# Moving the logits ahead of the second normalisation, and the slot statistics into the attention loop, in a fused Perceiver layer

## The chip, the cores and the metric

The kernel runs on one core of a Trainium2 chip. The metric is the time of one execution on the device, in microseconds (us); less is better. A core has a matrix engine (PE), a vector engine (DVE), an activation engine (ACT), a general engine (POOL) and a sync engine (SP) that only issues transfers. Each engine runs its own list of instructions in order, and they meet through semaphores.

## The reference, cut to what matters

One layer on x (128 rows of 256), with a context of 12544 rows of 256, in fp32:

```python
x = x + xattn(layernorm(x), ctx, W, b)          # softmax attention over 12544 context rows
x = x + conv(layernorm(x), proj_w, proj_b, filter_time)   # two stages of Fourier convolution and gating
x = x + soft_moe(layernorm(x), ...)
# soft_moe: a second layernorm on its input, with norm_g, norm_b
xn = (z - mean(z)) * rsqrt(var(z) + 1e-5) * norm_g + norm_b
se = ((s - mean(s)) * rsqrt(var(s) + 1e-5) * slot_g + slot_b) * scale     # 1024 slot rows of 256
logits = xn @ se.T                               # 128 x 1024
dispatch, combine = softmax over rows, softmax over slots
slots = dispatch.T @ xn                          # 1024 x 256
eout = (gelu(slots @ Wg + bg) * (slots @ Wu + bu)) @ Wd + bd     # 16 experts, 64 slots each
out = combine @ eout
```

## The kernel before, in words

The work has four stretches, one after the other.

The start (to about 10 us): x is normalised (`norm(0)`), transposed (`xhT`), W.T W is formed (`WW`), and the query `q_hi`, `q_lo` comes out of both. fp32 values are split in a high and a low part so that PE can use its fast fp32r form.

The attention loop: the context comes in 25 groups of 4 tiles of 128 rows (`raw`). Per group PE transposes the rows, ACT writes `cT_hi` and DVE `cT_lo` (`ctx_lo`), PE forms the scores, DVE takes the running maximum (`running_max`, which also writes `nsc`), ACT the exponentials (`prob`), PE transposes them, ACT and DVE split them (`prob_lo`), PE multiplies with the context rows (`weigh`), and DVE updates `O` (`update_output`). POOL and ACT split the context rows themselves (`c_hi`, `c_lo`). Steps are software-pipelined: step i works on groups i+1, i, i-1 and i-2. Steps 3 to 22 are a hardware loop of 5 turns with 4 steps each; steps 23 and up stand behind it.

The middle (about 111 to 129 us): residual, layernorm, projection, two stages of Fourier convolution, the residual `x2` and its statistics, the doubled layernorm (`rstd` from POOL's power, `xh`), the transposed `xnT`, the slot embeddings normalised by ACT (`se`, 8 tiles), transposed by PE and written to `seT` by ACT with the slot gains, then logits, dispatch and the first slots. The 8 slot tiles are dealt with in three pieces (tile 0, tiles 1 to 3, tiles 4 to 7).

The experts (from about 129 us): 8 pairs of experts; per pair the hidden products (`hidden_of`), gelu, the product, a transpose, the down product and the mix. Their weights, 3 MB a pair, stream in from SP's queue.

The order on every engine is written out by hand. The names that the change and the prediction touch:

```python
def slot_stats(loop, j):      # DVE: statistics of slot tile j; one per turn of the loop, three behind it
def slot_variance():          # DVE: 8 aggregates and the addition of EPS, in the middle
def slot_shift():             # DVE: the shift for normalising the slots, after POOL's power
def keep_busy(n):             # PE: n transposes that nothing reads
```

## Time and profile before

| | |
|---|---|
| time, median of 3 runs | 194.2 us (193.78 to 194.37) |
| the profiled execution's own time | 192.96 us |
| its span | 190.9 us |
| PE busy | 185.7 us (97%), 1268 instructions |
| DVE busy | 125.7 us (66%) |
| ACT busy | 108.9 us (57%) |
| POOL busy | 82.4 us (43%) |
| granted TensorE clock | 1.00 |

The span is what the profiler saw of the engines' work; 2.06 us of the execution lie around it. Busy shares are averages over stretches with different limits: PE is busy through the loop and the experts, while in the start and the middle some of its instructions are fillers (`keep_busy`) and the length is set by chains that go through several engines.

### The profile page before, as it was taken

Reading aid. Unit: us, or ns where it says so; the run is one execution under the profiler, and the core shown is the slowest. Engines: PE = TensorE matmul, PEld = TensorE weight load, DVE = VectorE, ACT = ScalarE, POOL = GpSimd, SP = SyncE. Lnnn points to the kernel's source line nnn. Section 1 sums busy time; section 2 is a strip of 40 time slices with the busy share of each in tenths; the row PEclk is TensorE's granted clock in tenths of the full one; section 3 lists DMA queues with packets and bytes.
Section 4 is the critical chain, followed back from the end, with each engine's and each line's share of the span. In section 5 each row is a group of like instructions: output and inputs, shape, how many; then the busy total and the mean of one; then the engine's idle time right before and its main releaser. Section 6 shows DMA issues by size and latency. Waiting matters only on the chain.

```text
span 190.9 us, 3968 instructions
## 1 busy us (share of the span) xinstructions
PE 185.7 (97%) x1268; PEld 145.5 (76%) x1268; DVE 125.7 (66%) x272; ACT 108.9 (57%) x226; POOL 82.4 (43%) x61
## 2 busy tenths in 40 slices
PE   6999999999999999999999999999999999999994
PEld 4888999999999999999999989974544555454463
DVE  3567988797777778777777888743673513515542
ACT  3568687677777767767776443967358521112210
POOL 2787978688777678877768012100000000000000
PEclk9999999999999999999999999999999999999999
DMA  5999957737784873984493399999999999993300
GB/s 185 321 347 367 357 177 277 256 129 232 246 276 142 281 248 116 353 236 150 135 240 91 124 352 385 353 374 367 382 365 383 280 353 289 273 208 99 75 0 27
DMA packets 25051, 47.01 MB, mean 246 GB/s; under 512 B 1616, under 2 KB 12112, under 8 KB 25040
## 3 DMA queue, kind: packets, MB, share of 16 engines
q1 hardware_dynamic: 23808, 43.52, 68.7%
q10 hardware_dynamic: 1232, 3.35, 7.2%
q8 instruction: 6, 0.10, 0.2%
q14 instruction: 5, 0.04, 0.1%
HBM read 46.73 MB, written 0.13 MB: 245 GB/s over the span
## 4 chain that ended last, share of the span: by engine, by line
PE 93%; ACT 2%; DMA 2%; DVE 1%; issue 0%; SPq 0%; ACTq 0%
PE bank L662 15%; PE bank L413 11%; PE bank L676 6%; PE bank L454 6%; PE bank L458 6%; PE bank L456 6%; PE bank L426 6%; PE bank L430 6%; PE bank L428 6%; PE bank L439 6%; PE bank L724 2%; PE bank L714 2%; PE bank L549 2%; DMA W_sb<-in_L_xattn_W_dram 2%; PE bank L568 2%; ACT seT L881 1%
## 5 line engine op out<-in xcount | busy, mean ns | idle before, releaser
L998 POOL TENSOR_TENSOR c_lo<-raw,c_hi 128x1024 fp32r<-128x1024 f32 (+1 forms) x25 | 54.0, 2160 | 20.1 <-ACT c_hi L793 20.1
L1076 DVE TENSOR_TENSOR cT_lo<-bank,cT_hi 128x512 fp32r<-128x512 f32 (+1 forms) x50 | 31.7, 675 | 10.6 <-ACT cT_hi L820 9.5
L820 ACT ACTIVATE cT_hi<-bank 128x512 fp32r<-128x512 f32 (+1 forms) x48 | 25.7, 584 | 10.1 <-PE bank L413 10.1
L454 PE MATMUL bank<-c_hi,pT_hi 128*128 128x258 f32 x98 | 29.9, 305 | 0.0
L458 PE MATMUL bank<-c_hi,pT_lo 128*128 128x258 f32 x98 | 27.7, 282 | 0.0
L456 PE MATMUL bank<-c_lo,pT_hi 128*128 128x256 f32 x98 | 27.5, 281 | 0.0
L993 POOL TENSOR_TENSOR c_hi<-raw,zero 128x512 fp32r<-128x512 f32 (+1 forms) x25 | 25.7, 1027 | 1.4 <-DMA raw<-in_ctx_dram 1.4
L413 PE MATMUL bank<-tab,raw 128*128 128x128 f32 x196 | 25.8, 273 | 0.2 <-DVE cT_lo L1076 0.2
L827 ACT ACTIVATE pT_hi<-bank 128x512 fp32r<-128x512 f32 (+1 forms) x25 | 14.7, 590 | 14.2 <-PE bank L439 14.1
L413 PEld LDWEIGHTS bank<-tab,raw 128*128 128x128 f32 x196 | 22.1, 141 | 0.9 <-issue 0.3
L426 PE MATMUL bank<-cT_hi,q_hi 128*128 128x512 f32 (+1 forms) x50 | 21.5, 430 | 0.0
L1088 DVE TENSOR_SCALAR_CACHE_REDUCE nsc<-bank,s,negm 128x512 f32<-128x512 f32 (+1 forms) x25 | 19.8, 793 | 0.8 <-PE bank L430 0.7
L1094 DVE TENSOR_TENSOR pT_lo<-bank,pT_hi 128x512 fp32r<-128x512 f32 (+1 forms) x25 | 17.0, 679 | 4.2 <-ACT pT_hi L827 3.9
L835 ACT ACTIVATE prob<-nsc,negm 128x512 f32<-128x512 f32 (+1 forms) x25 | 17.8, 710 | 3.3 <-DVE nsc L1088 2.9
L430 PE MATMUL bank<-cT_hi,q_lo 128*128 128x512 f32 (+1 forms) x50 | 19.5, 389 | 0.0
L428 PE MATMUL bank<-cT_lo,q_hi 128*128 128x512 f32 (+1 forms) x50 | 19.3, 386 | 0.0
L456 PEld LDWEIGHTS bank<-c_lo,pT_hi 128*128 128x128 f32 x98 | 18.7, 190 | 0.0
L458 PEld LDWEIGHTS bank<-c_hi,pT_lo 128*128 128x128 f32 x98 | 18.5, 189 | 0.0
L454 PEld LDWEIGHTS bank<-c_hi,pT_hi 128*128 128x128 f32 x98 | 18.5, 189 | 0.0
L793 ACT ACTIVATE c_hi<-raw 128x512 fp32r<-128x512 f32 (+1 forms) x25 | 15.6, 624 | 0.0
L662 PE MATMUL bank<-early_gu,slots_or_se 128*64 128x512 f32 x64 | 15.2, 600 | 0.0
L1104 DVE SCALAR_TENSOR_TENSOR O<-O,alpha,bank 128x258 f32<-128x258 f32 x25 | 12.0, 482 | 4.4 <-PE bank L458 3.1
(178 smaller groups left out, 289.7 us busy)
## 6 DMA issues: line engine op xcount, KB each, us to landing
raw<-in_ctx_dram SPq DMA_DIRECT2D x24, 512.0 KB, 3.8
bias<-biases_dram ACTq DMA_DIRECT2D x10, 320.0 KB, 7.5
late_gu<-in_L_ffn_Wg_dram SPq DMA_DIRECT2D x3, 1024.0 KB, 10.7
late_gu<-in_L_ffn_Wu_dram SPq DMA_DIRECT2D x3, 1024.0 KB, 11.2
late_d<-in_L_ffn_Wd_dram SPq DMA_DIRECT2D x3, 1024.0 KB, 13.6
early_gu<-in_L_ffn_Wg_dram SPq DMA_DIRECT2D x4, 512.0 KB, 4.9
early_gu<-in_L_ffn_Wu_dram SPq DMA_DIRECT2D x4, 512.0 KB, 4.6
early_d<-in_L_ffn_Wd_dram SPq DMA_DIRECT2D x4, 512.0 KB, 4.9
```

Source lines behind the costliest of these rows:

```text
L413: last = nc.tensor.transpose(bank[h][:, t * P:(t + 1) * P], raw[:, slot, t, h * P:(h + 1) * P], ident)
L426: nc.tensor.matmul(bank[2 + r][:, 0:n], q_hi[:, h, :], cT_hi[:, r, h, 0:n], start=(h == 0), stop=False)
L428: nc.tensor.matmul(bank[2 + r][:, 0:n], q_hi[:, h, :], cT_lo[:, r, h, 0:n], start=False, stop=False)
L430: last = nc.tensor.matmul(bank[2 + r][:, 0:n], q_lo[:, h, :], cT_hi[:, r, h, 0:n], start=False, stop=(h == DK - 1))
L454: nc.tensor.matmul(bank[6 + r][:, 0:D + 2], ph, c_hi[:, slot, t, :], start=(t == 0), stop=False)
L456: nc.tensor.matmul(bank[6 + r][:, 0:D], ph, c_lo[:, slot, t, :], start=False, stop=False)
L458: last = nc.tensor.matmul(bank[6 + r][:, 0:D + 2], pl, c_hi[:, slot, t, :], start=False, stop=(t == nt - 1))
L662: last = nc.tensor.matmul(bank[b][a * SL:(a + 1) * SL, :], slotsT[:, k, p * P + a * SL:p * P + (a + 1) * SL], w_gu(s, which, a, a + 1)[:, ...
L820: nc.scalar.activation(cT_hi[:, g % 2, h, 0:n], bank[h][:, 0:n], ACT.Copy).then_inc(cThi_rdy, 1)
L993: nc.gpsimd.tensor_tensor(c_hi[:, slot, 0:nt // 2, 0:D], raw[:, slot, 0:nt // 2, :], zero[:, 0:1].unsqueeze(2).broadcast_to([P, nt // 2, D ...
L998: nc.gpsimd.tensor_tensor(c_lo[:, slot, 0:nt, :], raw[:, slot, 0:nt, :], c_hi[:, slot, 0:nt, 0:D].bitcast(fp32), ALU.subtract).then_inc(cl ...
L1076: nc.vector.tensor_tensor(cT_lo[:, g % 2, h, 0:n], bank[h][:, 0:n], cT_hi[:, g % 2, h, 0:n].bitcast(fp32), ALU.subtract).then_inc(cTlo_rdy, 1)
```

## The change

What it does, part by part:

- The logits are no longer computed from the finished `xnT`, but from x2 less its mean, transposed. norm_g, slot_g and scale are multiplied into the slots' columns (`slot_columns`, on DVE, ahead of the copy to `xhT`), and the factor `rstd` and the share of norm_b (a row of 1024 numbers, one a slot) come in where DVE takes the logits out of PSUM (`finish_logits`).
- The share of norm_b: DVE multiplies the slots with slot_g*scale*norm_b in the loop (`slot_dot`), sums that row (`row_sum`), combines (`beta`); PE transposes it to 8 rows, ACT copies it, stores it to DRAM as 8 lines of 512 bytes and loads it back, spread over 128 partitions, into `comb`. The row that `slot_dot` needs goes through DRAM in the same way at the start.
- The slot statistics are all taken in the loop (2 a turn); `slot_variance` and `row_sum` stand right behind the loop, `slot_shift` in the last group's step.
- ACT normalises the first four slot tiles ahead of the copies to `xhT`, and writes the first piece of `seT` early. Two small steps of DVE go to ACT and POOL (`p_sb`'s third part, `x1`).
- Tile 0's logits go through the same path as the others'; the products with a diagonal and with ones are gone. `logits(2)` is cut in pieces, one of which stands ahead of `gather(0)`.

```diff
@@ DVE, the start
             norm(0, x_sb[:, :], xh[:, :], xh_rdy)
+            def slot_columns():
+                dve.wait_ge(ld_scale, 16)
+                link(nc.vector.tensor_scalar(col[:, 1:3, :], col[:, 1:3, :], scale_b[:, 0:1], None, ALU.mult))
+                nc.vector.tensor_tensor(b_col[:, :], col[:, 1, :], col[:, 4, :], ALU.mult).then_inc(bcol_rdy, 1)
+                dve.wait_ge(bcol_rdy, 1)
+                for i in (1, 2):
+                    last = nc.vector.tensor_tensor(col[:, i, :], col[:, i, :], col[:, 3, :], ALU.mult)
+                last.then_inc(gs_rdy, 1)
+
+            slot_columns()
             dve.wait_ge(xhT_ps, 1)
             nc.vector.tensor_copy(xhT[:, :, :].rearrange("p k t -> p (k t)"), bank[XH_BANK[0]][:, 0:D]).then_inc(xhT_rdy, 1)
@@ DVE, slots
+            def slot_dot(loop, j):
+                dve.wait_ge(ld_brow, 16)
+                dve.wait_ge(bdot_rdy, loop * 2 + (1 if j == 0 else 2))
+                nc.vector.scalar_tensor_tensor(out=junk, in0=se[:, bass.ds(loop + j, 1), :].rearrange("p j d -> p (j d)"),
+                                               scalar=1.0, in1=b_row, op0=ALU.mult, op1=ALU.mult,
+                                               accum_out=bdot[:, bass.ds(loop + j, 1)]).then_inc(bdot_rdy, 1)
+            def row_sum():
+                dve.wait_ge(bdot_rdy, 2 * LOOPS + 1)
+                nc.vector.tensor_scalar(junk, b_row, -1.0, 0.0, ALU.mult, ALU.add, accum_out=b_neg[:, 0:1]
+                                        ).then_inc(bdot_rdy, 1)
             def slot_shift():
-                dve.wait_ge(rstd_rdy, 3)
+                dve.wait_ge(rstd_rdy, 2)
                 nc.vector.scalar_tensor_tensor(out=se_shift, in0=se_mv[:, :, 0], scalar=-1.0, in1=se_rstd[:, :],
                                                op0=ALU.mult, op1=ALU.mult).then_inc(shift_rdy, 1)
+                dve.wait_ge(bdot_rdy, 2 * LOOPS + 2)
+                link(nc.vector.scalar_tensor_tensor(out=beta[:, :], in0=se_mv[:, :, 0], scalar=b_neg[:, 0:1],
+                                                    in1=bdot[:, :], op0=ALU.mult, op1=ALU.add))
+                nc.vector.tensor_tensor(beta[:, :], beta[:, :], se_rstd[:, :], ALU.mult).then_inc(beta_rdy, 1)
@@ DVE, the loop and behind it
-            dve.wait_ge(ld_scale, 16)
-            for i in (1, 2):
-                last = nc.vector.tensor_scalar(col[:, i, :], col[:, i, :], scale_b[:, 0:1], None, ALU.mult)
-            last.then_inc(gs_rdy, 1)
             with dve.Fori(0, LOOPS) as n:
                 for u in range(RING):
                     step(n, FIRST + u)
-                    if u == 0:
-                        slot_stats(n, 0)
+                    if u < 2:
+                        slot_stats(n, 3 * u)
+                    else:
+                        slot_dot(n, 3 * (u - 2))
+            slot_variance()
+            row_sum()
@@ DVE, the middle
+            nc.vector.tensor_scalar(x_sb[:, :], x2[:, :], mv[:, 0:1], None, ALU.subtract).then_inc(xc_rdy, 1)
+            dve.wait_ge(xcT_ps, 1)
+            nc.vector.tensor_copy(xnT[:, 0, :], bank[XC_BANK[0]][:, 0:P]).then_inc(xcT_rdy[0], 1)
+            def finish_logits(n):
+                lo, hi = PIECES[n]
+                dve.wait_ge(L_ps, n + 1)
+                dve.wait_ge(ld_beta, 16)
+                nc.vector.scalar_tensor_tensor(out=comb[:, lo * P:hi * P], in0=bank[L_BANK[n]][:, 0:(hi - lo) * P],
+                                               scalar=rstd[:, 0:1], in1=comb[:, lo * P:hi * P],
+                                               op0=ALU.mult, op1=ALU.add).then_inc(L_rdy, 1)
@@ PE
+                if i == GROUPS:
+                    pe.wait_ge(beta_rdy, 1)
+                    nc.tensor.transpose(bank[3][0:PAIRS, 0:P], beta[:, :], ident).then_inc(betaT_ps, 1)
-            transposed_logits()
-            first_logits()
+            pe.wait_ge(seT_rdy, 2)
+            for k in range(DK):
+                pe.wait_ge(xcT_rdy[k], 1)
+                logits(0, (k,))
             logits(1, (0,))
-            shift_logits()
+            transpose_logits(0)
             logits(1, (1,))
+            transpose_dispatch(0)
+            pe.wait_ge(seT_rdy, 4)
+            logits(2, (0,), 0)
             gather(0)
-            dispatch_sums()
             transpose_logits(1)
@@ ACT, the middle
+            act.wait_ge(betaT_ps, 1)
+            nc.scalar.activation(beta_j, bank[3][0:PAIRS, 0:P], ACT.Copy).then_inc(betaT_rdy, 1)
+            act.wait_ge(betaT_rdy, 1)
+            act.dma_start(rows_dram[0:SLOTS].rearrange("(j p) -> j p", p=P), beta_j).then_inc(st_beta, 16)
+            normalise((0, 1, 2, 3))
+            act.wait_ge(st_beta, 16)
+            act.dma_start(comb[:, :], rows_dram[0:SLOTS].rearrange("(a n) -> a n", a=1).broadcast_to([P, SLOTS])
+                          ).then_inc(ld_beta, 16)
             for k in range(DK):
                 act.wait_ge(xhT_ps, k + 2)
                 nc.scalar.activation(xhT[:, k, :], bank[XH_BANK[1][k]][:, 0:P], ACT.Copy).then_inc(xhT_rdy, 1)
+            spectrum(0)
             spectrum(1)
```

The order on DVE at the start, before: the copy to `xhT` follows the normalised `xh`.

```order
L1036 TENSOR_SCALAR xh<-x_sb,mv,rstd 128x256 [waits rstd_rdy]
L1046 COPY xhT<-bank 128x256 [waits xhT_ps]
L1048 TENSOR_SCALAR WW<-bank 128x257 [waits WW_ps]
L1076 TENSOR_TENSOR cT_lo<-bank,cT_hi 128x512 [waits cThi_rdy] x2
L1125 SCALAR_TENSOR_TENSOR q_lo<-bank,WW,q_hi 128x128 [waits qhi_rdy,WW_rdy]
```

And in the changed kernel (`dve_n` and `bcol_rdy` are counted up by DVE's own instructions):

```order
L1053 TENSOR_SCALAR xh<-x_sb,mv,rstd 128x256 [waits rstd_rdy]
L1066 TENSOR_SCALAR col<-col,scale_b 128x4 [waits ld_scale]
L1067 TENSOR_TENSOR b_col<-col 128x2 [waits dve_n]
L1070 TENSOR_TENSOR col<-col 128x2 [waits bcol_rdy]
L1070 TENSOR_TENSOR col<-col 128x2
L1075 COPY xhT<-bank 128x256 [waits xhT_ps]
L1077 TENSOR_SCALAR WW<-bank 128x257 [waits WW_ps]
```

Four small instructions and a wait for the load of `scale` now stand ahead of `xhT` and `WW`.

The order on DVE behind the loop, before; the first row is the last group's `ctx_lo`, the second group 23's `running_max`:

```order
L1076 TENSOR_TENSOR cT_lo<-bank,cT_hi 128x256 [waits cThi_rdy] x2
L1088 TENSOR_SCALAR nsc,negm<-bank,s,negm 128x512 [waits prob_rdy,negm_rdy,score_ps]
L1094 TENSOR_TENSOR pT_lo<-bank,pT_hi 128x512 [waits pThi_rdy]
L1104 SCALAR_TENSOR_TENSOR O<-O,alpha,bank 128x258 [waits O_upd,pv_ps,alpha_rdy]
L1054 BN_STATS se_stat<-slots_or_se 128x6
```

In the changed kernel, from the last `slot_dot` of the loop on:

```order
L1091 SCALAR_TENSOR_TENSOR p_sb,bdot<-slots_or_se,p_sb 128x256
L1185 REGISTER_ALU
L1185 COMPARE_AND_BRANCH
L1103 BN_AGGR se_mv<-se_stat 128x2 [waits stat_rdy]
L1103 BN_AGGR se_mv<-se_stat 128x2 x7
L1105 TENSOR_SCALAR se_mv<-se_mv 128x8 [waits dve_n]
L1097 TENSOR_SCALAR p_sb,b_neg<-p_sb 128x256 [waits bdot_rdy]
L1120 TENSOR_TENSOR cT_lo<-bank,cT_hi 128x256 [waits cThi_rdy] x2
L1132 TENSOR_SCALAR nsc,negm<-bank,s,negm 128x512 [waits prob_rdy,negm_rdy,score_ps]
```

The aggregates, the addition and the row's sum now stand ahead of the last `ctx_lo` and of group 23's `running_max`.

The order on ACT between the attention and the projection, in the changed kernel (before, the copies to `xhT` stood third behind `pT_hi`):

```order
L828 ACTIVATE pT_hi<-bank 128x256 [waits pv_ps,pT_ps]
L889 ACTIVATE p_sb<-bank 8x128 [waits betaT_ps]
L891 DMA rows_dram<-p_sb 8x128 [waits betaT_rdy]
L877 ACTIVATE slots_or_se<-slots_or_se,se_stat,se_rstd 128x256 [waits shift_rdy]
L877 ACTIVATE slots_or_se<-slots_or_se,se_stat,se_rstd 128x256 x3
L895 DMA comb<-rows_dram 128x1024 [waits st_beta]
L899 ACTIVATE xhT<-bank 128x128 [waits xhT_ps] x2
```

The copies to `xhT` now stand behind a store, four normalised tiles and the wait for the store's landing.

## Rows read from the trace of the kernel before

**Rows 1.** The page's chain of work that ended last, share by engine.

```profile
PE 93%; ACT 2%; DMA 2%; DVE 1%; issue 0%; SPq 0%; ACTq 0%
```

**Rows 2.** Timeline of the start: start, duration (us), engine, line, operation, [idle before].

```profile
5.92 1.04 POOL L993 TENSOR_TENSOR c_hi<-raw,zero 128x512 fp32r<-128x512 f32 x1 [1.39 <-DMA raw<-in_ctx_dram]
5.94 0.42 DVE L1046 COPY xhT<-bank 128x256 f32<-128x256 f32 x1 [0.96 <-PE bank L265]
...
6.81 0.42 DVE L1048 TENSOR_SCALAR WW<-bank 128x257 f32<-128x257 f32 x1 [0.45 <-PE bank L388]
7.03 2.19 POOL L998 TENSOR_TENSOR c_lo<-raw,c_hi 128x1024 fp32r<-128x1024 f32 x1
...
7.48 1.06 PE L477 MATMUL bank<-xhT,WW 128*128 128x128 f32 x8
```

**Rows 3.** Timeline of ACT's queue at the start.

```profile
1.69 0.47 ACTq L777 DMA_DIRECT2D scale_b<-in_L_ffn_scale_dram  x1
```

**Rows 4.** Transfers by line: size of one, median us from issue to landing.

```profile
bias<-biases_dram ACTq DMA_DIRECT2D x10, 320.0 KB, 7.5
...
out_dram<-x SPq DMA_DIRECT2D x2, 64.0 KB, 1.6
...
scale_b<-in_L_ffn_scale_dram ACTq DMA_DIRECT2D x1, 0.5 KB, 4.3
```

**Rows 5.** Timeline of DVE and POOL around 20 us.

```profile
18.56 2.20 POOL L998 TENSOR_TENSOR c_lo<-raw,c_hi 128x1024 fp32r<-128x1024 f32 x1 [0.16 <-ACT c_hi L793]
...
20.36 1.41 DVE L1138 TENSOR_SCALAR col<-col,scale_b 128x2 f32<-128x2 f32 x2
20.71 1.04 POOL L993 TENSOR_TENSOR c_hi<-raw,zero 128x512 fp32r<-128x512 f32 x1
```

**Rows 6.** Line 1138 alone: duration in ns, least, median, most.

```profile
L1138 DVE TENSOR_SCALAR col<-col,scale_b x2: 419/750/1082, 20.4 to 20.7; 128x2 f32<-128x2 f32 x2
```

**Rows 7.** Timeline of DVE around 114 us, the slots' variance.

```profile
113.32 0.64 DVE L1063 BATCH_NORM_AGGREGATE se_mv<-se_stat 128x2 f32<-128x6 f32 x8
113.99 0.17 DVE L1065 TENSOR_SCALAR se_mv<-se_mv 128x8 f32<-128x8 f32 x1
```

**Rows 8.** Timeline of DVE in one step of the loop.

```profile
77.30 0.48 DVE L1104 SCALAR_TENSOR_TENSOR O<-O,alpha,bank 128x258 f32<-128x258 f32 x1 [0.17 <-PE bank L458]
78.31 1.29 DVE L1076 TENSOR_TENSOR cT_lo<-bank,cT_hi 128x512 fp32r<-128x512 f32 x2 [0.53 <-ACT cT_hi L820]
```

**Rows 9.** Timelines of POOL, DVE, ACT and PE behind the loop.

```profile
103.45 1.19 POOL L998 TENSOR_TENSOR c_lo<-raw,c_hi 128x512 fp32r<-128x512 f32 x1 [0.51 <-ACT c_hi L793]
...
103.95 0.81 DVE L1088 TENSOR_SCALAR_CACHE_REDUCE nsc<-bank,s,negm 128x512 f32<-128x512 f32 x1 [0.43 <-PE bank L430]
...
104.88 0.71 ACT L835 ACTIVATE prob<-nsc,negm 128x512 f32<-128x512 f32 x1
...
106.34 0.60 PE L439 MATMUL bank<-tab,prob 128*128 128x128 f32 x4
```

**Rows 10.** Timelines of ACT, DVE and PE in the middle.

```profile
112.77 0.45 ACT L870 ACTIVATE xhT<-bank 128x128 f32<-128x128 f32 x2 [0.21 <-PE bank L271]
...
122.27 2.79 ACT L881 ACTIVATE seT<-bank,col 128x512 f32<-128x512 f32 x4 [0.44 <-PE bank L529]
...
123.08 0.15 DVE L1208 TENSOR_SCALAR mv<-mv 128x1 f32<-128x1 f32 x1
...
127.97 0.61 PE L625 MATMUL bank<-disp,xn 128*128 128x128 f32 x4
...
129.19 1.94 PE L662 MATMUL bank<-early_gu,slots_or_se 128*64 128x512 f32 x8
131.06 1.98 PE L568 MATMUL bank<-seT,xnT 128*128 128x512 f32 x4
```

**Rows 11.** Timeline of PE: its first instructions, and some at 114 us.

```profile
1.20 2.93 PE L383 MATMUL bank<-O 128*128 128x256 f32 x6 [1.20 <-DVE O L1039]
...
114.15 1.03 PE L518 MATMUL bank<-pw,xhT 128*128 128x256 f32 x4
```

More of the change, by code:

```diff
@@ L502, in _, with transpose_slots @@
                 spectrum(o)
-            keep_busy(1)
+            pe.wait_ge(betaT_rdy, 1)
             transpose_xh(pe, 1)
+            def transpose_slots(n):
+                k, half = SE_PIECE[n]
+                pe.wait_ge(se_rdy, 4 * (half + 1))
+                if n == 3:
+                    pe.wait_ge(seT_rdy, 2)
+                for j in range(4):
+                    last = nc.tensor.transpose(bank[SE_BANK[n]][:, j * P:(j + 1) * P],
+                                               se[:, 4 * half + j, k * P:(k + 1) * P], ident)
+                last.then_inc(seT_ps, 1)
+            transpose_slots(0)
             pe.wait_ge(ld_pw, 32)
@@ L551, in _ @@
                     last.then_inc(conv_ps, 1)
[L552 removed]
+            for n in range(1, 4):
                 transpose_slots(n)
[L554 to L557 removed]
+            keep_busy(3, 4)
+            pe.wait_ge(xc_rdy, 1)
             for k in range(DK):
[L559 to L562 removed]
@@ L563, in _, with logits @@
-            pe.wait_ge(seT_rdy, 4)
-            def logits(n, chunks=range(DK)):
+                nc.tensor.transpose(bank[XC_BANK[k]][:, 0:P], x_sb[:, cols(k)], ident).then_inc(xcT_ps, 1)
+            keep_busy(2, 4)
+            def logits(n, chunks=range(DK), part=None):
                 lo, hi = PIECES[n]
+                lo, hi = (lo * P, hi * P) if part is None else (lo * P + part * 2 * P, lo * P + (part + 1) * 2 * P)
+                at = lo - PIECES[n][0] * P
                 for k in chunks:
-                    last = nc.tensor.matmul(bank[L_BANK[n]][:, 0:(hi - lo) * P], xnT[:, k, :],
-                                            seT[:, k, lo * P:hi * P], start=(k == 0), stop=(k == DK - 1))
-                if k == DK - 1:
+                    last = nc.tensor.matmul(bank[L_BANK[n]][:, at:at + hi - lo], xnT[:, k, :],
+                                            seT[:, k, lo:hi], start=(k == 0), stop=(k == DK - 1))
+                if k == DK - 1 and part != 0:
@@ L865, in _, with normalise, slots_evacuated @@
                 step(None, i)
-            spectrum(0)
+            def normalise(tiles):
+                act.wait_ge(shift_rdy, 1)
+                for j in tiles:
+                    nc.scalar.activation(se[:, j, :], se[:, j, :], ACT.Identity, scale=se_rstd[:, j:j + 1],
+                                         bias=se_shift[:, j:j + 1]).then_inc(se_rdy, 1)
+            def slots_evacuated(n):
+                act.wait_ge(gs_rdy, 1)
+                act.wait_ge(seT_ps, n + 1)
+                k, half = SE_PIECE[n]
+                nc.scalar.activation(seT[:, k, half * 512:(half + 1) * 512], bank[SE_BANK[n]][:, :],
+                                     ACT.Identity, scale=col[:, 1, k:k + 1], bias=col[:, 2, k:k + 1]
+                                     ).then_inc(seT_rdy, 1)
+            act.wait_ge(betaT_ps, 1)
[6 more added lines that the diff above has]
+                          ).then_inc(ld_beta, 16)
             for k in range(DK):
```

208 lines of the change are left out of this document (91 added, 117 removed).

## The prediction

> **What bounds the kernel now.** I read the page's chain of waits first: 93% of what ended last runs through PE [rows 1]. So every microsecond by which the stream of real PE work is pushed back counts in full, and so does each by which it is brought forward. Then I read the timelines where the change sits. There are three places, and at all of them PE waits for a chain through other engines: the start, where the query is formed from `xhT` and `WW` [rows 2]; the steps behind the loop, where each group must pass DVE, ACT and PE in turn [rows 9]; and the middle, between x2 and the first expert product [rows 10]. In the middle the reader should see two chains side by side: x2's statistics end at 123.23, while ACT still writes the four pieces of `seT` from 122.27 to 125.06. The later of the two lets the logits start; gather(0) follows at 127.97 and the first expert product at 129.19.
>
> **The middle: a gain of 1.5 us.** Behind the statistics (123.23) the changed kernel needs the centring (estimate 0.35, a 256-wide operation), PE's transposes (0.4 to their end) and the copies (0.3): logits from about 124.35, no longer behind POOL's power. ACT is in time, since one piece of `seT` and half of the normalising have moved forward. From there: two products for tile 0 (0.44 plus 0.15 until PSUM is readable), `finish_logits` 0.3, transpose 0.3, maximum 0.3, exponential with its sum 0.55, transpose back 0.3, copy 0.3: gather(0) at about 127.2 where it was at 127.97. The copies of `slots` follow as before (0.65 later), and the expert product at about 128.25 in place of 129.19, because nothing else stands between now. Gain 0.95. Next, `logits(2)` took about 1.9 behind that product (131.06, four records [rows 10]); a quarter, 0.47, now lies ahead of gather(0) in a wait, and one transpose of 0.11 is gone. Sum: 0.95 + 0.47 + 0.11 = 1.5 us. The short steps are estimates from neighbours of the same width; I take 1.0 to 2.0 as its bounds.
>
> **The wait for the store on ACT: 0.2 us.** The copies to `xhT` (112.77, [rows 10]) now stand behind the store of `beta`, four normalised tiles (an estimate of 0.5 apiece, 256 wide) and the store's landing. The store is issued about 3.3 us before the copies are wanted. Landing has no row of its own: the final stores land in 1.6 us with nothing beside them, a small load beside large ones took 4.3 [rows 4]. With its successor's issue (0.47 [rows 3]) the wait costs nothing below 3 us and 1.2 at 4.3. I take 0.2, between the ends. The load that follows has 12 us; the bias loads of 320 KB on that queue, beside the same weights, need 7.5 [rows 4], so 512 KB should land in time.
>
> **Behind the loop: a loss of 1.4 us.** Ahead of `ctx_lo` and group 23's `running_max` now stand the last `slot_dot`, eight aggregates (0.64) and the addition (0.17) [rows 7], and `row_sum` (0.5, as wide as the update of O, 0.48 [rows 8]). By their lengths alone they end near 104.4, and the maximum (103.95, with 0.43 idle ahead of it) would start at 105.1. But the addition is a TENSOR_SCALAR that reads and writes SBUF, and POOL works on `c_lo` until 104.64 [rows 9]. What this means is seen around 20 us [rows 5, 6]: two such operations on 2 columns took 419 and 1082 ns where a like one took 0.17 [rows 7], and they ended at 20.78 and 21.79, just where POOL's operations ended (18.56 + 2.20 = 20.76, 20.71 + 1.04 = 21.75). DVE was held until POOL let go. So the addition ends at 104.67, `row_sum` at 105.1, `ctx_lo` at 105.9, the maximum at 106.65, the exponential (0.71) at 107.45, and PE's transposes, which stood at 106.34, start at 107.5: 1.2 late. They were the last thing waited for there, and everything on PE comes behind them. The transposed `beta` adds 0.11, and changes of pace 0.1. I take 1.4; if nothing is held it is 0.7.
>
> **In the loop: nothing.** Each `slot_dot` (0.5) meets an idle 0.53 ahead of `ctx_lo` [rows 8]. If it is held by a POOL operation of 1.04, `ctx_lo` ends 0.6 later, still more than half a microsecond before PE overwrites its bank one step (about 4 us) on; the two steps in four without a dot make it good. Without this cover each dot would cost up to 0.6, 6 us in all; that is the price if I misread the slack.
>
> **The start: a loss of 3.3 us.** This is the largest term. `slot_columns` stands ahead of the copy to `xhT`, which was at 5.94, and of `WW`, 6.81 [rows 2]. It waits for `scale`: issued at 1.69, landed 4.3 later, at 5.99 [rows 3, 4]. Its first instruction is the very one that was held there [rows 5, 6], and POOL has been in `c_hi` since 5.92: held until 6.96. The next, a TENSOR_TENSOR with both inputs in `col`, may start at about 7.03, and POOL starts `c_lo` at 7.03, for 2.19. Whoever loses that race, one of the three small products waits until 9.22, and POOL's next `c_hi` (1.04) follows at once and holds the next until 10.25, as the second one in rows 5 was held. Then `xhT` starts near 10.3, `WW` ends at 11.1, and PE forms the query at 11.1, not 7.48. A part of that, 0.3 by estimate, is made good, as DVE was idle for some tenths between these steps. So 3.3 us, all of it behind which PE works without a gap. The bounds: the lengths alone (four times 0.15 to 0.17, with waits) give 6.7, within 0.1 of what WW waits for anyway; the first instruction held alone gives 7.4 and 0.6 us; one of the products slipping through gives 2.4. I take the upper case since the nearest row by tile, width and place is the one that was held. Against it stands that DVE's operations with one input in PSUM, as `cT_lo` in rows 8, run beside POOL at their normal length, so it is not every operation.
>
> The Trainium skill bears on exactly this point: the page "SBUF — State Buffer" (section "SBUF: two separate sides") says that DVE and GpSimd share a port pair by an exclusive lock held for a whole instruction, taken by DVE for operations in a two-port mode and also for those with two SBUF inputs while GpSimd reads SBUF. The held TENSOR_SCALAR of rows 5 agrees; that two-input products are held too, no row here shows. By that rule the start costs the 3.3 us of the sum; if it held for one-input operations only, the 0.6 us.
>
> **The sum.** +3.3 (start) + 1.4 (behind the loop) + 0.2 (store) - 1.5 (middle) = +3.4 us. The profiled execution took 192.96 us, 2.06 of them around its span, and would take 196.4. The median of the runs shown is 1.2 us above it; I add the difference to the median: 194.2 + 3.4 = 197.6.
>
> **The rivals.**
> 1. Only one-input operations are held. Start +0.6, behind the loop +1.4, store +0.2, middle -1.5: +0.7, 194.9 us. For it: rows 5 show no two-input product. Against: both have all operands in SBUF. Chance 0.17.
> 2. The gain wins, faster: at the start nothing is held because `scale` lands early enough and the products are too small to matter (+0.1), behind the loop only the lengths count (+0.7), store 0.2, middle -1.5: -0.5, 193.7 us. It decides as soon as start and tail together cost less than 0.7. Against it: rows 5, where two columns waited 1.08 us. With a middle that gains 2.0 it is 193.2. Chance 0.13.
> 3. As forecast, and PE's clock drops besides. PE would stand still from 7.5 to 11.1. The granted clock is 1.00 in every stretch before, but PE's first six records took 2.93 us where four of the same width later take 1.03 [rows 11], about 0.44 against 0.22 apiece: the lower of its levels, 1.2 and not 2.4 GHz, after having done nothing. If it falls back in the gap, up to eight records of the query and the first scores run at half speed: another 0.9 to 1.7 us, 198.5 to 199.3. Chance 0.12.
> 4. As forecast: 196.9 to 198.2, chance 0.58.
>
> **How the numbers follow.** A measurement of this kernel tells a difference of about 0.3%, 0.6 us. Faster than 193.6: most of rival 2 and some of a larger gain in rival 1, 0.14. Between 193.6 and 194.8: the rest of those, 0.12. Slower: 0.74. The range 194.7 to 199.2 takes in the forecast, most of rivals 1 and 3, and leaves out rival 2: 0.82. Under the forecast alone it would be 196.6 to 198.6.
>
> **What the profile after would show.** DVE's three products at the start at 1 to 2 us each, ending with POOL's operations, and `xhT` near 10.3; if they take 0.15, rival 1 or 2. The steps of the loop still as far apart as before, with `slot_dot` at 0.5 to 1.2. PE idle for about a microsecond ahead of the transposes of group 23. On ACT a gap ahead of the second transfer. From the copies to `xhT` to the second expert product 1.5 us less than before. The forecast fails if the products at the start aren't held, if a dot delays PE in the loop, or if `comb`'s load lands after 126 us plus the shift, which would stall the logits.

## The result and the profile after

| | before | changed |
|---|---|---|
| time, median (range) of 4 runs each | 193.99 us (193.68 to 194.37) | 197.63 us (195.62 to 198.06) |
| ratio, 95% interval | | 1.0172 (1.0123 to 1.0221) |
| profiled execution, its span | 192.96, 190.9 us | 198.06, 196.0 us |

The change costs 3.6 us, where 3.4 were forecast on 194.2 (197.6). The four runs of the changed kernel lie 2.4 us apart, and the profiled one is the slowest: its span is 5.1 us above that of before. Part of its excess is a slow clock of PE in the start, which is in some of the profiles below and not in others. The ratios leave out the slowest runs of a kernel, the medians don't.

The page's chain, shares by engine, answers to [rows 1]:

```profile
PE 31%; DMA 7%; ACT 2%; DVE 1%; issue 1%; ACTq 0%; DVEq 0%
PE bank L663 11%; DMA bias<-biases_dram 5%; PE bank L677 4%; DMA rows_dram<-p_sb 2%; PE bank L574 2%; PE bank L715 2%; PE bank L592 2%; PE bank L725 1%; PE bank L563 1%; PE bank L694 1%; PE bank L552 1%; PE bank L609 1%; PE bank L626 1%; PE bank L544 1%; PE bank L534 1%
```

Its shares add up to 42%, 82 us of 196: it was followed back to about 114 us, and its oldest link is a transfer, `rows_dram<-p_sb`, the store of `beta`. Such a link was not in the chain before. The timeline of ACT shows it ([rows 10] for before):

```profile
113.24 0.29 ACTq L891 DMA_DIRECT2D rows_dram<-p_sb  x1
113.58 2.08 ACT L877 ACTIVATE slots_or_se<-slots_or_se,se_stat,se_rstd 128x256 f32<-128x256 f32 x4 [0.37 <-ACT p_sb L889]
118.00 0.33 ACTq L895 DMA_DIRECT2D comb<-rows_dram  x1
118.38 0.45 ACT L899 ACTIVATE xhT<-bank 128x128 f32<-128x128 f32 x2 [2.73 <-DMA rows_dram<-p_sb]
```

The store took 4.76 us from issue to the end of the wait, and ACT stood idle for 2.73. PE, whose transposes were at 116.49, waited:

```profile
116.49 0.44 PE L284 MATMUL bank<-tab,xh 128*128 128x128 f32 x2
118.80 1.13 PE L544 MATMUL bank<-pw,xhT 128*128 128x128 f32 x8 [1.44 <-ACT xhT L899]
```

The start, timelines of DVE, POOL and PE, answers to [rows 2]; the last row is PE in the kernel before:

```profile
6.82 0.95 DVE L1066 TENSOR_SCALAR col<-col,scale_b 128x4 f32<-128x4 f32 x1 [1.81 <-DMA scale_b<-in_L_ffn_scale_dram]
7.81 0.16 DVE L1067 TENSOR_TENSOR b_col<-col 128x2 f32<-128x2 f32 x1
8.01 2.14 DVE L1070 TENSOR_TENSOR col<-col 128x2 f32<-128x2 f32 x2
10.07 0.41 DVE L1075 COPY xhT<-bank 128x256 f32<-128x256 f32 x1
...
6.71 1.04 POOL L1006 TENSOR_TENSOR c_hi<-raw,zero 128x512 fp32r<-128x512 f32 x1 [2.15 <-DMA raw<-in_ctx_dram]
7.89 2.17 POOL L1011 TENSOR_TENSOR c_lo<-raw,c_hi 128x1024 fp32r<-128x1024 f32 x1
10.03 1.03 POOL L1006 TENSOR_TENSOR c_hi<-raw,zero 128x512 fp32r<-128x512 f32 x1
...
4.72 2.08 PE L403 MATMUL bank<-W_sb 128*128 128x257 f32 x4 [0.60 <-DMA W_sb<-in_L_xattn_W_dram]
8.66 1.04 PE L428 MATMUL bank<-tab,raw 128*128 128x128 f32 x8
10.87 1.16 PE L496 MATMUL bank<-xhT,WW 128*128 128x128 f32 x8 [1.18 <-DVE WW L1077]
...
4.55 1.14 PE L388 MATMUL bank<-W_sb 128*128 128x257 f32 x4 [0.42 <-DMA W_sb<-in_L_xattn_W_dram]
```

Two things are to be seen. On DVE the scaling ends with `c_hi` (6.71 + 1.04 = 7.75), and the first product of the pair with `c_lo` (7.89 + 2.17 = 10.06): both were held. The product `b_col` got in between (0.16), and so did the second one of the pair, behind `c_lo` (0.15). On PE, four matmuls 257 wide took 2.08 us where the same four took 1.14 before: the clock was at its lower level, 1.2 GHz, until about 8.6, and the context's transposes, at 6.61 in the kernel before, began at 8.66. So of the 3.39 us by which the query is late [rows 2], 2.05 would be there without a column.

Behind the loop, DVE, POOL and PE ([rows 9]; the steps of the loop bring a shift of 3.13 with them):

```profile
106.96 0.85 DVE L1105 TENSOR_SCALAR se_mv<-se_mv 128x8 f32<-128x8 f32 x1
107.72 0.41 DVE L1097 TENSOR_SCALAR_CACHE_REDUCE p_sb<-p_sb 128x256 f32<-128x256 f32 x1
...
108.72 0.80 DVE L1132 TENSOR_SCALAR_CACHE_REDUCE nsc<-bank,s,negm 128x512 f32<-128x512 f32 x1
...
106.59 1.19 POOL L1011 TENSOR_TENSOR c_lo<-raw,c_hi 128x512 fp32r<-128x512 f32 x1 [0.51 <-ACT c_hi L794]
...
110.34 0.66 PE L454 MATMUL bank<-tab,prob 128*128 128x128 f32 x4 [0.51 <-ACT prob L836]
```

The addition (0.17 in [rows 7]) took 0.85 and ended with `c_lo`, at 107.8. PE's transposes come at 110.34, 4.00 later than before: 0.87 more than the shift.

For all profiles the same marks on PE's timeline were read: the first scores, the last transposes of context, the spectrum, the V projection, the first expert product, the first transposes of `hid`, the span's end. The table gives the length of each segment less that of the kernel before, in us (for before: 10.52, 91.41, 8.69, 2.57, 16.00, 7.74, 53.97):

| profiled execution | to scores(0) | loop | behind loop | to V proj. | to expert | to `hid` | experts | sum |
|---|---|---|---|---|---|---|---|---|
| changed | 3.14 | -0.01 | 1.01 | 1.47 | -0.28 | -0.53 | 0.30 | 5.1 |
| s_two_late | 0.74 | 0.02 | 1.01 | 2.29 | 1.38 | -0.53 | -0.01 | 4.9 |
| s_all_late | 2.76 | 0.07 | 1.01 | 1.44 | -0.27 | -0.53 | 0.52 | 5.0 |
| s_reload_late | 2.52 | 0.00 | 1.00 | -0.07 | -0.27 | -0.54 | -0.04 | 2.6 |
| s_tail_late | 3.11 | 0.01 | 0.25 | 3.83 | 2.21 | -0.53 | 0.02 | 8.9 |
| w_before | 0.05 | 0.00 | 0.03 | -0.01 | 0.00 | 0.00 | 0.03 | 0.1 |
| w_after | 2.30 | 0.01 | 1.00 | 1.16 | -0.28 | -0.54 | 0.05 | 3.7 |
| m_three | 0.86 | 0.10 | 0.24 | 0.93 | -0.35 | -0.53 | 0.05 | 1.3 |
| m_three_warm | 1.31 | 0.08 | 0.25 | 0.93 | -0.34 | -0.54 | 0.01 | 1.7 |
| b_probe | 2.80 | 3.34 | 0.03 | -0.01 | 0.00 | 0.00 | 0.04 | 6.2 |
| b_columns | 3.69 | 1.68 | 0.00 | -0.01 | 0.01 | -0.01 | 0.04 | 5.4 |
| m_four | 2.76 | 0.09 | 0.24 | -0.11 | -0.28 | -0.53 | 0.03 | 2.2 |
| m_four_warm | 1.32 | 0.07 | 0.24 | -0.11 | -0.27 | -0.53 | 0.28 | 1.0 |

### The profile page after: what moved, and what is told of

It is laid out like the page before. It is cut to its first block and busy times, and to the rows that moved or that the text cites. A ratio compares the mean times of both kernels' runs of the same rounds, so it can differ in the third digit from the quotient of the medians.

```text
span 196.0 us, 4028 instructions
## 1 busy us (share of the span) xinstructions
PE 187.1 (95%) x1261; PEld 146.1 (75%) x1261; DVE 137.5 (70%) x303; ACT 109.4 (56%) x227; POOL 82.9 (42%) x61
## 5 line engine op out<-in xcount | busy, mean ns | idle before, releaser
L1006 POOL TENSOR_TENSOR c_hi<-raw,zero 128x512 fp32r<-128x512 f32 (+1 forms) x25 | 25.6, 1024 | 2.1 <-DMA raw<-in_ctx_dram 2.1
L454 PE MATMUL bank<-tab,prob 128*128 128x128 f32 x98 | 14.8, 273 | 0.5 <-ACT prob L836 0.5
```

Of the source, the lines that this page charges most:

```text
L1006: nc.gpsimd.tensor_tensor(c_hi[:, slot, 0:nt // 2, 0:D], raw[:, slot, 0:nt // 2, :], zero[:, 0:1].unsqueeze(2).broadcast_to([P, nt // 2, D ...
```

## The experiments

The kernel before ran beside each group of kernels; its medians were 193.6 us (first four), 193.46 (next four), 193.36 (next three) and 194.0 (last).

**s_two_late.** The two products by `norm_g` go to where the kernel before scaled its columns.

```diff
                 nc.vector.tensor_tensor(b_col[:, :], col[:, 1, :], col[:, 4, :], ALU.mult).then_inc(bcol_rdy, 1)
-                dve.wait_ge(bcol_rdy, 1)
-                for i in (1, 2):
-                    last = nc.vector.tensor_tensor(col[:, i, :], col[:, i, :], col[:, 3, :], ALU.mult)
-                last.then_inc(gs_rdy, 1)
...
+            dve.wait_ge(bcol_rdy, 1)
+            for i in (1, 2):
+                last = nc.vector.tensor_tensor(col[:, i, :], col[:, i, :], col[:, 3, :], ALU.mult)
+            last.then_inc(gs_rdy, 1)
             dve.wait_ge(ld_se, 16)
             with dve.Fori(0, LOOPS) as n:
```

> The changed kernel, with the two products of the columns by norm_g (the second TENSOR_TENSOR pair of slot_columns) moved from ahead of the xhT copy to where the kernel before had its column scaling, ahead of the loop; the scaling and b_col stay at the start. Theory A (small VectorE operations with both inputs in SBUF wait for a GpSimd operation that is running, as the 2.14 us of this pair from 8.01 until c_lo's end at 10.06 in the changed kernel's trace suggest): the xhT copy starts about 2.1 us sooner, the query matmuls too, and the time falls from 197.6 by 1.8 to 2.2, to about 195.6. Rival B (only operations with one input are held, the pair itself takes 0.15 to 0.3 us, and the late query of the changed kernel is due to later loads and a slower start): within 0.3 of 197.6.

Measured: 196.7 us (194.58 to 198.38), ratio 1.0107 (1.0064 to 1.0150). The start did what theory A says: query at 8.13, 2.7 sooner than in the changed kernel's profile and 1.9 sooner than in that of w_after below, whose clock was up early. The total didn't: 196.7 lies between the 195.6 of theory A and the 197.3 at which rival B begins. The profiled execution, 197.85 and so 1.2 above the median, gave the gain back further on. The store of `beta` took 5.58 us (issued 110.87, next issue on ACT 116.45), PE idled 2.26 ahead of the V projection, and then its clock fell:

```profile
117.25 1.13 PE L544 MATMUL bank<-pw,xhT 128*128 128x128 f32 x8 [2.26 <-ACT xhT L899]
118.22 1.69 PE L552 MATMUL bank<-pw,xhT 128*128 128x256 f32 x4
```

The same four records, L518 before, took 1.03 in [rows 11]. The windows (PE's busy time, then other engines', granted clock, DMA share) say it outright:

```profile
115.00:118.00 3.00, 0.74 (x7) 0.78 (x7) 0.16 (x1) 1.17 (x5) 0.54 (x1) 1.00 0.92 330
118.00:122.00 4.00, 4.00 (x18) 3.60 (x17) 1.71 (x6) 1.47 (x4) 0.00 (x0) 0.57 1.04 400
```

In the table this is the +1.38 to the expert where the others have -0.28: 1.66 us for one gap. In how many of the other eleven runs the clock fell is not shown.

**s_all_late.** All of `slot_columns` stands behind `q_lo`; transpose, copy, store and reload of `b_col` follow it.

```diff
-            slot_columns()
             dve.wait_ge(xhT_ps, 1)
...
+            slot_columns()
             dve.wait_ge(s0_ps, 1)
             nc.vector.tensor_copy(s0[:, :], bank[5][:, 0:1]).then_inc(s0_rdy, 1)
```

> The changed kernel, with all of slot_columns moved behind q_lo (VectorE idles there until s0), the b_col transpose behind scores of group 0, its copy behind the first running_max, its store and reload behind the steps that they stood ahead of. Theory A (the start is worth +3.1 to +3.3): the query matmuls start at 7.5 to 8.0 as before and the time is about 194.4 (194.0 to 194.9), some 1.1 us better than with the pair alone moved. Rival B (the start's delay is mostly that of loads or of the TensorE's slow first matmuls and would be there without the columns): 196.5 or more. Rival C (the operations moved are held at their new place, and s0, running_max and the first group come late by as much): 196 or more, with the query early and scores of group 1 late.

Measured: 195.69 us (194.85 to 197.99), ratio 1.0096 (1.0056 to 1.0137). The profiled execution, 197.99, looked like rival B: no column stands ahead of the query any more, and it still starts at 10.38. Its PE timeline:

```profile
4.66 2.08 PE L403 MATMUL bank<-W_sb 128*128 128x257 f32 x4 [0.53 <-DMA W_sb<-in_L_xattn_W_dram]
6.96 1.92 PE L403 MATMUL bank<-W_sb 128*128 128x257 f32 x4
8.67 1.88 PE L428 MATMUL bank<-tab,raw 128*128 128x128 f32 x8
10.38 1.07 PE L496 MATMUL bank<-xhT,WW 128*128 128x128 f32 x8
```

PE ran at 1.2 GHz until about 10.4. The start can be late for two reasons that overlap, and the changed kernel's profile had both. Six of the twelve runs stood at 194.85 to 195.4, five at 196.6 to 198: the lower ones lie at the upper end of theory A's 194.0 to 194.9 and above it, the median between the two theories. The profile settles rival C all the same, and prices the columns. At their new place POOL stands still (from 10.99 to 13.93), and the same four operations take 0.61 us in all, none of them held:

```profile
12.35 0.22 DVE L1066 TENSOR_SCALAR col<-col,scale_b 128x4 f32<-128x4 f32 x1
12.61 0.16 DVE L1067 TENSOR_TENSOR b_col<-col 128x2 f32<-128x2 f32 x1
12.80 0.23 DVE L1070 TENSOR_TENSOR col<-col 128x2 f32<-128x2 f32 x2
```

**s_reload_late.** ACT issues the reload into `comb` behind the `xhT` copies and the spectra.

```diff
-            act.wait_ge(st_beta, 16)
-            act.dma_start(comb[:, :], rows_dram[0:SLOTS].rearrange("(a n) -> a n", a=1).broadcast_to([P, SLOTS])
-                          ).then_inc(ld_beta, 16)
             for k in range(DK):
                 act.wait_ge(xhT_ps, k + 2)
...
             spectrum(1)
+            act.wait_ge(st_beta, 16)
+            act.dma_start(comb[:, :], rows_dram[0:SLOTS].rearrange("(a n) -> a n", a=1).broadcast_to([P, SLOTS])
+                          ).then_inc(ld_beta, 16)
```

> The changed kernel, with ScalarE's wait for the beta store and the issue of the comb reload moved behind the xhT copies and the two spectra. Theory A (the 2.73 us idle of ScalarE ahead of the xhT copies sets the V projection, 1.5 us late): the projection starts some 1.5 us sooner, the reload lands by 126 and is wanted at 130, the time is about 196.1 (195.8 to 196.4). Rival B (what the wait costs is given back: the bias and weight loads, or the slot pipeline behind it, end last in the middle anyway): 197.2 or more.

Measured: 195.54 us (193.95 to 198.57), ratio 1.0068 (1.0030 to 1.0105). The V projection comes 2.50 behind the spectrum where it came 4.04, nothing is given back later, and the profiled time is 195.58. Theory A, with a median 0.3 below its range. By the medians, which are of different groups, the saving is 2.1 and not 1.5; a fall of the clock that goes with the gap, as in s_two_late, may be the rest, but no run here parts it off. The start of this profile holds a gap too: PE idled 2.42 us for the columns, and the clock stayed up behind it.

```profile
10.25 1.16 PE L496 MATMUL bank<-xhT,WW 128*128 128x128 f32 x8 [2.42 <-DVE WW L1077]
11.24 1.04 PE L428 MATMUL bank<-tab,raw 128*128 128x128 f32 x8
```

**s_tail_late.** Variance, `row_sum` and shift move behind the maxima, the `beta` transpose behind the last weighing.

```diff
-            slot_variance()
-            row_sum()
             for i in range(FIRST + RING * LOOPS, GROUPS + 2):
                 step(None, i)
...
                 if i == LAST:
-                    slot_shift()
+                    slot_variance()
                 if 1 <= i <= GROUPS:
                     prob_lo(loop, i - 1, (GT if full else tiles_of(i - 1)) * P)
+                if i == GROUPS:
+                    row_sum()
+                    slot_shift()
```

> The changed kernel, with the eight bn_aggr and the TENSOR_SCALAR behind the running_max of the last group, row_sum and slot_shift behind prob_lo of the last group, and the beta transpose behind the last weighing. Theory A (these operations ahead of running_max(23), one of them held by c_lo until 107.78, made the transposes of the probabilities 0.9 to 1.0 late): the time falls by 0.6 to 1.0, to about 196.8, less up to 0.4 given back because bn_aggr now stands ahead of prob_lo(23), which has 0.46 us of idle. Rival B (VectorE has no room anywhere in the last steps, or beta late makes the store late and the wait on ScalarE longer): within 0.3 of 197.6.

Measured: 200.16 us (198.6 to 202.28), ratio 1.0278 (1.0209 to 1.0348), the slowest of all. The segment behind the loop shrank as theory A says, from +1.01 to +0.25. But `beta` is stored later, at 114.49, ACT got on at 119.59, PE idled 2.74, and the clock was down for longer:

```profile
115.00:120.00 5.00, 1.76 (x11) 1.12 (x9) 1.53 (x8) 1.97 (x5) 0.54 (x1) 0.87 0.98 356
120.00:125.00 5.00, 4.61 (x17) 4.28 (x18) 0.68 (x2) 2.61 (x7) 0.00 (x0) 0.50 1.05 392
```

The second half of rival B was right, but not its price (within 0.3 of 197.6). Against the changed kernel's segments the later store costs 2.36 us (3.83 less 1.47) and the clock 2.49 (2.21 and 0.28).

**w_before, w_after.** One matmul more in the opening filler, in the kernel before and in the changed one.

```diff
                 nc.tensor.matmul(bank[7][:, 0:D], O[:, 0:P], O[:, 0:D], start=True, stop=True)
+            nc.tensor.matmul(bank[7][:, 0:P], O[:, 0:P], O[:, 0:P], start=True, stop=True)
```

> The kernel before, with one matmul of 128x128 more in TensorE's opening filler on zeros, so that the filler ends where W_sb lands (4.5 to 4.7) and not 0.4 to 0.6 us ahead of it. The five profiles of changed kernels so far differ in the start: where the idle gap ahead of L403 was 0.37 to 0.42 us, four matmuls of 128x257 took 1.14 us, where it was 0.53 to 0.60, 2.08 us, TensorE's half rate, and it stayed so until 8.5 to 10.4. Theory G (the gap decides whether the clock rises now or later): with the gap closed every execution starts at the full rate, the few runs of before at 194.9 to 195.6 vanish, the median is within 0.3% of before (193.3 to 193.7) and the scatter below 1 us. Rival H (the moment at which the clock rises is chance, or the filler has no part in it): the same share of runs stays 1.5 to 2.5 us late.

> The changed kernel, with the same matmul more in the filler. It parts the two causes of the late query in the changed kernel's profile, where TensorE was at half rate until about 8.6 (square_W, xh and ctx transposes 2.05 us late) and the columns' chain on VectorE ended after that (1.34 us more). Theory A (columns held by GpSimd cost 3.1 to 3.3 also where TensorE runs at full rate, since the xhT copy waits for c_lo's end): the query starts at 10.3 to 10.9 with L403 at 1.1 us, the time stays at 197 to 197.6. Rival B (the columns add to the slow clock but cost little at the full one): query at 8.5 to 9.0, time about 195.5.

Measured: w_before 193.43 us (192.81 to 194.55), 0.9984 (0.9945 to 1.0023); w_after 196.61 us (195.37 to 199.8), 1.0137 (1.0078 to 1.0196). w_after's profile has the changed start at nearly full clock, DVE, POOL and PE:

```profile
6.04 0.94 DVE L1067 TENSOR_SCALAR col<-col,scale_b 128x4 f32<-128x4 f32 x1 [1.15 <-DMA scale_b<-in_L_ffn_scale_dram]
7.02 0.16 DVE L1068 TENSOR_TENSOR b_col<-col 128x2 f32<-128x2 f32 x1
7.21 2.10 DVE L1071 TENSOR_TENSOR col<-col 128x2 f32<-128x2 f32 x2
9.23 0.41 DVE L1076 COPY xhT<-bank 128x256 f32<-128x256 f32 x1
...
7.04 2.19 POOL L1012 TENSOR_TENSOR c_lo<-raw,c_hi 128x1024 fp32r<-128x1024 f32 x1
9.18 1.04 POOL L1007 TENSOR_TENSOR c_hi<-raw,zero 128x512 fp32r<-128x512 f32 x1
...
4.42 1.47 PE L404 MATMUL bank<-W_sb 128*128 128x257 f32 x4
10.03 1.16 PE L497 MATMUL bank<-xhT,WW 128*128 128x128 f32 x8 [2.18 <-DVE WW L1078]
```

Query 2.55 late, scores 2.30 late, with PE waiting 2.18 for DVE: the columns' own price. `b_col` began 0.02 us ahead of `c_lo` and was not held. Both figures lie somewhat under theory A's (query at 10.3 to 10.9, 197 to 197.6), and further from rival B's (8.5 to 9.0, 195.5). w_before does as the kernel before does, though its scatter, 1.7 us, is not under the 1 us of theory G.

**b_columns.** The kernel before with the four column operations of the change ahead of `xhT`; its own two, ahead of the loop, are gone.

```diff
             norm(0, x_sb[:, :], xh[:, :], xh_rdy)
+            dve.wait_ge(ld_scale, 16)
+            link(nc.vector.tensor_scalar(col[:, 1:3, :], col[:, 1:3, :], scale_b[:, 0:1], None, ALU.mult))
+            link(nc.vector.tensor_tensor(diag[:, 0:2], col[:, 1, :], col[:, 4, :], ALU.mult))
+            for i in (1, 2):
+                last = nc.vector.tensor_tensor(diag[:, 2 * i:2 * i + 2], col[:, i, :], col[:, 3, :], ALU.mult)
+            last.then_inc(gs_rdy, 1)
```

> The kernel before, with only the four column operations of the change's slot_columns (scaling, b_col's product, two products by norm_g) on VectorE ahead of the xhT copy, their results unused but for the scaling; its own two column scalings ahead of the loop are gone. Nothing else of the change is in it: no store, no reload, no beta. Theory A (small operations with two SBUF inputs, and the scaling, wait for running GpSimd operations; at TensorE's full rate this made the query 2.55 us late in w_after): query at 9.8 to 10.1, time 2.3 to 2.7 above before, about 195.9. Rival B (the delay needs the store or the loads of the change, or is the clock's): query at 8.0 to 8.5, time 193.7 to 194.3. The forecast's third branch (only one-input operations held) gave +0.7: 194.2.

Measured: 195.89 us (194.11 to 198.97), 2.5 above before by the medians; ratio 1.0076 (1.0023 to 1.0130). Six of its 13 runs stood at 197.9 to 199. Its profile shows the query at 10.14, 2.66 late, with the matmuls of `W` at full rate (1.14): theory A, and the columns alone do it. The profiled execution, 198.34, is one of the six, and what lifts it came behind:

```profile
6.00:10.00 4.00, 1.84 (x13) 1.45 (x12) 3.78 (x6) 1.91 (x4) 3.89 (x3) 1.00 0.91 350
10.00:14.00 4.00, 3.86 (x23) 3.86 (x24) 1.94 (x5) 2.44 (x5) 0.33 (x1) 0.67 1.06 359
14.00:18.00 4.00, 4.00 (x14) 3.31 (x15) 2.10 (x5) 0.01 (x1) 3.18 (x2) 0.50 0.17 59
18.00:22.00 4.00, 4.00 (x26) 3.48 (x25) 2.79 (x7) 3.62 (x7) 1.44 (x1) 0.98 0.91 285
```

PE idled 2.30 for the columns and its clock then fell to half: 3.69 late at the scores, 1.68 more in the loop. This is rival 3 of the prediction. That it is what lifts the other five as well is likely by their times, but no trace shows it.

**b_probe.** The kernel before with twelve operations of two columns ahead of its scalings (and one line that fills their inputs with ones).

```diff
+            for r in range(4):
+                nc.vector.tensor_tensor(diag[:, 32 + 8 * r:34 + 8 * r], diag[:, 0:2], diag[:, 2:4], ALU.mult)
+                nc.vector.tensor_scalar(diag[:, 34 + 8 * r:36 + 8 * r], diag[:, 4:6], scale_b[:, 0:1], None, ALU.mult)
+                nc.vector.tensor_copy(diag[:, 36 + 8 * r:38 + 8 * r], diag[:, 6:8])
             for i in (1, 2):
```

> The kernel before, with twelve small operations (128x2) on VectorE ahead of its column scalings at 20.4, four times in turn: TENSOR_TENSOR of two SBUF inputs, TENSOR_SCALAR with a per-partition scalar, COPY. They run while GpSimd works on c_hi (20.7 to 21.7) and c_lo (22.0 to 24.2). Theory A (held from a GpSimd operation's start to its end, whatever the form): one of the twelve takes about 1 us and ends with c_hi, the next few run at 0.15 in the gap, one more ends with c_lo. Rival B (only one or two of the three forms are held): the others run at 0.15 to 0.2 in the middle of a GpSimd operation.

Measured: one run, 199.13 us, of whose 6.2 us 2.8 are a slow clock at the start and 3.3 the twelve operations. DVE, then POOL:

```profile
23.48 1.08 DVE L1140 TENSOR_SCALAR diag<-diag,scale_b 128x2 f32<-128x2 f32 x1
...
24.82 0.15 DVE L1139 TENSOR_TENSOR diag<-diag 128x2 f32<-128x2 f32 x1
24.89 2.17 DVE L1140 TENSOR_SCALAR diag<-diag,scale_b 128x2 f32<-128x2 f32 x1
...
27.04 1.01 DVE L1139 TENSOR_TENSOR diag<-diag 128x2 f32<-128x2 f32 x1
...
23.51 1.03 POOL L993 TENSOR_TENSOR c_hi<-raw,zero 128x512 fp32r<-128x512 f32 x1
24.82 2.21 POOL L998 TENSOR_TENSOR c_lo<-raw,c_hi 128x1024 fp32r<-128x1024 f32 x1 [0.28 <-ACT c_hi L793]
26.98 1.05 POOL L993 TENSOR_TENSOR c_hi<-raw,zero 128x512 fp32r<-128x512 f32 x1
...
29.16 1.25 PE L413 MATMUL bank<-tab,raw 128*128 128x128 f32 x8 [3.02 <-DVE cT_lo L1077]
```

Both forms are held, the one-input TENSOR_SCALAR (1.08, 2.17) and the two-input TENSOR_TENSOR (1.01), each until the end of POOL's operation; what starts in a gap of POOL takes 0.15 to 0.22. No COPY began well inside a running operation, so of it nothing is shown. PE idled 3.02 us for all this, and its clock did not fall: the windows behind read 1.00.

**m_three, m_three_warm, m_four, m_four_warm.** m_three joins the moves of s_all_late and s_tail_late with the reload into `comb` behind `slots_evacuated(0)`; the kernels with warm in the name have the longer filler too. m_four's further move:

```diff
+            normalise((0, 1, 2, 3))
             act.wait_ge(betaT_ps, 1)
             nc.scalar.activation(beta_j, bank[3][0:PAIRS, 0:P], ACT.Copy).then_inc(betaT_rdy, 1)
...
-            normalise((0, 1, 2, 3))
```

> The changed kernel with three moves together: slot_columns behind q_lo (as in s_all_late), the comb reload behind slots_evacuated(0), and the tail's operations as in s_tail_late. Theory A with the segments of the last four profiles (tail +0.25 in place of +1.01, store wait 0, middle -0.7 to -0.9, start 0 at full clock, loop 0): 193.2 where TensorE starts at full rate, about 196 where it doesn't, in two groups. Rival B (mends don't add up: beta or its reload lands late and logits wait, or bias loads end last in the experts, +0.6): 194 and more even for the lower group.

> The same three moves and the longer filler. Theory G with A: every run in the lower group, 192.8 to 193.4 with a scatter under 1 us, 0.2 to 0.5% faster than before. Rival H: two groups 2 to 3 us apart as without it. Rival B as for m_three: 194 or more.

> m_three with one move more on ScalarE: normalise of slots 0 to 3 ahead of the beta copy and its store, since in m_three's trace it stood behind them and made the xhT copies (114.68, transposes done at 113.9) and the V projection 0.93 late. Theory A: the V projection comes 2.5 to 2.6 behind the spectrum as in the kernel before, time 192.3 to 192.8 for the lower group of runs, 0.2 to 0.4% faster than before, and middle and experts as in m_three. Rival B: the beta store, now 0.7 later, lands so late that ScalarE waits for it ahead of the p_sb copy at 118 to 119 and gives 0.3 to 1 back: 193 to 193.6.

> m_four with the longer filler of w_before. So far the upper group of runs (2 us and more above the lower) had 2 of 12 runs in m_three, 6 of 12 in m_four, 17 of 81 in the kernel before, and none of 24 in w_before and m_three_warm, though in m_three_warm's profile L403 ran at half rate (2.08 us) with no idle ahead of it. Theory G2 (the filler does not set when the clock rises, but spares the latest rises): no run above 194.5, median 193.2 to 193.8, within 0.3% of before. Rival H (chance alone, the filler does nothing): a quarter to a half of the runs above 195. That the four moves beat the kernel before by 0.3 to 0.5% in the lower group (segments of m_four's profile: -0.53 behind scores of group 0) would show as runs at 192.4 to 192.6.

Measured: m_three 193.98 us (193.28 to 195.92), 1.0024 (0.9989 to 1.0060); m_three_warm 194.31 (193.62 to 194.9), 1.0016 (0.9979 to 1.0052); m_four 194.45 (192.9 to 195.93), 1.0002 (0.9946 to 1.0057); m_four_warm 193.54 (193.02 to 195.44), 0.9969 (0.9928 to 1.0009). In m_three's profile the query stands at 8.33, 0.85 late, as much as the slow first matmuls of `W` account for (2.08 for 1.14): at the new place the columns cost PE nothing, though POOL holds the first of them there (0.49). The moves take all of the loss back and end level with the kernel before: the last is 0.46 us below it by the medians, within what can be told. Behind the scores m_four is 0.56 us shorter than before by the table; runs at 192.4 to 192.6, which that would give at before's start, were not seen.

The filler did not do what theory G said. In m_three_warm PE had no idle ahead of `W`'s matmuls and still took 2.08 for them; b_columns idled 0.62 and took 1.14. So the gap does not decide. That the longer filler spares the latest rises is likelier than not: of the kernel before, 24 of 98 runs were above 194.8 us, of w_before, m_three_warm and m_four_warm together 2 of 36. But the kernels differ, the bound of 194.8 was picked with the runs in sight, m_four_warm has a run at 195.44 where theory G2 allows none above 194.5, and w_after, with the longer filler too, still spreads over 4.4 us. It was not settled.

## Why the prediction was right, point by point

The total, the sign and the order of the terms held. The terms are read at full clock, from w_after where that matters.

- **Start, +3.3 forecast, +2.3 measured** (2.52 in s_reload_late). The mechanism held: operations held until POOL's end, both forms. The step that was mis-sized is the last hold, "until 10.25". The first product slipped in between `c_hi` and `c_lo`, the second was held by `c_lo`, and the third got through at 9.2 beside the start of the next `c_hi`: one hold less, 1 us. The prediction had this very case among its bounds ("one of the products slipping through gives 2.4") and took the upper one. That two-input products are held, which no row of before showed, b_probe (1.01 us) and b_columns (2.10 for the pair) show; rival 1 is refuted. The Trainium skill ("SBUF — State Buffer", section "SBUF: two separate sides") says that a DVE operation with two SBUF inputs, too, is blocked while a GpSimd (POOL) operation that reads SBUF has the port pair they share; these rows agree.
- **Loop, 0 forecast, -0.01 measured.** The dots were held, as the prediction allowed: that of 101.58 took 1.03 and ended at 102.61, 0.28 behind POOL's operation; the last one, 0.64 long, ended 0.28 behind one too (106.36 and 106.08). The slack covered them. What a dot takes unheld, no row shows.
- **Behind the loop, +1.4 forecast, +1.0 measured**, in five profiles alike. The addition was held as forecast; `row_sum` took 0.41, and of the 0.21 for the beta transpose and pace at most 0.14 is seen.
- **Wait for the store, +0.2 forecast, +1.2 to +2.3 measured** (four profiles with `beta` where the change has it). This step failed in size. The wait ended 4.4 (w_after) to 5.6 us (s_two_late) after the issue, with the DMA engines' share at 0.92 to 1.04: all above the upper bound of landing, 4.3. I had gone by a value between that and the lower bound, 1.6, that of the final stores, which land with nothing beside them. The sum was also off in itself: by its own 3.3 and 0.47 us the wait costs nothing below 2.8, and 1.5 at 4.3, not 1.2. And I had not thought that this gap too can drop the clock: 1.66 and 2.5 us more in two profiles.
- **Middle, -1.5 forecast, -0.8 to -0.9 measured** in each profile that has the change and no fall. Behind the first expert product it went as forecast: -0.53 for 0.58. The gain of 0.95 up to the first expert product was 0.28. The logits started 1.50 behind the statistics (130.35), not 1.12, because PE's centring transposes stood behind the last slots' transposes, which waited for ACT's `seT`, and fillers; and from there to gather it took 3.09, not 2.85.
- **Experts, 0 forecast, +0.3 in the changed kernel's profile**, 0.0 to 0.5 elsewhere, with a `bias` load in the chain. In the changed kernel that load took 9.73 us, from 160.12 on; the median of ACT's loads of `bias` is 6.8. DVE formed `hid` late by it, and PE idled 0.23 once, at 172.34 (0.48 in s_all_late). Why the loads land at different times stays open.
- **Rival 3, the clock**, was given 0.12. It fell behind the query's gap in b_columns, not in w_after, s_reload_late or the changed kernel's profile, and in the middle in two profiles. Where it fell at the start it cost about 3 us (1.4 and 1.68), not the 0.9 to 1.7 of the prediction.

At full clock the measured terms add up to 2.3 + 1.0 + 1.2 - 0.8 = +3.7 (w_after), the forecast's to +3.4: four terms were off by 0.4 to 1.0 each, two each way, and they balanced. That the total came within 0.3 us is luck.

## What to carry to other kernels

Before small DVE operations on SBUF are put on a critical path, look at what POOL runs at that moment: each can cost the rest of POOL's operation, however few columns it has, and a place a few microseconds on may be free. Before an engine is made to wait for its own store, count 5 us when the DMA engines are full, and put behind that wait nothing that PE wants. And price a new idle gap of PE twice: once for the gap, once for the clock that may, or may not, fall behind it.
